# Scores computed a second time, transposed, with the row maxima contracted in, in place of transposed probabilities

## The reference

```
qkv = (h @ Wqkv.T).reshape(b, n, 3, H, HD)
q = _ln(qkv[:, :, 0].transpose(0, 2, 1, 3), qn_g, qn_b)
k = _ln(qkv[:, :, 1].transpose(0, 2, 1, 3), kn_g, kn_b)
v = qkv[:, :, 2].transpose(0, 2, 1, 3)
scores = jnp.einsum('bhnd,bhmd->bhnm', q, k) / jnp.sqrt(jnp.float32(HD))
attn = jax.nn.softmax(scores, axis=-1)
o = jnp.einsum('bhnm,bhmd->bhnd', attn, v)
x = x + o.transpose(0, 2, 1, 3).reshape(b, n, H * HD) @ Wout.T
```

## Time and profile before

| | |
|---|---|
| median of 3 runs | 466.15 us (465.32 to 466.54) |
| profiled execution | 464.51 us |
| its span, first to last instruction | 462.8 us |
| PE busy | 421.9 us, 91% |
| ACT, DVE, POOL busy | 311.0, 295.8, 154.8 us |
| mean granted TensorE clock | 0.978 of full |

### The profile page before, as it was taken

One profiled execution on the slowest core, in us unless ns is written; L12 is line 12 of the kernel. 1 busy time (PEld: TensorE's weight loads), 2 busy tenths in 40 slices (PEclk: granted clock), 3 DMA queues, 4 the chain that ended last, 5 costly groups with the idle time before them and its releaser, 6 DMA issues.

```text
span 462.8 us, 9105 instructions
## 1 busy us (share of the span) xinstructions
PE 421.9 (91%) x2990; PEld 366.4 (79%) x2990; DVE 295.8 (64%) x727; ACT 311.0 (67%) x697; POOL 154.8 (33%) x127
## 2 busy tenths in 40 slices
PE   1979878769999999999999999999999986889996
PEld 1567557658998998999999899999998875668794
DVE  2555545547776777677767767776776554886233
ACT  2345626566878887887788788778877766765531
POOL 6200313126553455355345535543553200100000
PEclk9999999889999999999999999999999999599999
DMA  7400000191000000000000000000000000000001
GB/s 212 131 1 1 2 0 1 32 339 39 1 4 0 1 1 0 0 0 0 0 0 0 0 0 0 0 0 0 0 0 2 1 0 2 0 1 1 1 1 45
DMA packets 7492, 9.49 MB, mean 21 GB/s; under 512 B 371, under 2 KB 4270, under 8 KB 7470
## 3 DMA queue, kind: packets, MB, share of 16 engines
q1 hardware_dynamic: 5646, 7.11, 5.1%
q10 hardware_dynamic: 1824, 2.10, 1.6%
HBM read 8.68 MB, written 0.52 MB: 20 GB/s over the span
## 4 chain that ended last, share of the span: by engine, by line
PE 71%; DVE 5%; issue 1%; ACT 1%; POOL 1%; DVEq 0%; ACTq 0%
PE pair L1349 24%; PE bank L1130 12%; PE pair L1315 8%; PE pair L1333 6%; PE pair L1334 6%; PE pair L1130 5%; PE pair L1539 1%; PE pair L1445 1%; PE pair L1484 1%; PE pair L1520 1%; PE bank L1484 1%; PE pair L1501 1%; PE pair L1528 1%; PE bank L1528 1%; PE bank L1520 1%
## 5 line engine op out<-in xcount | busy, mean ns | idle before, releaser
L1349 PE MATMUL pair<-v_s,probs_T 128*128 128x128 f32 x1024 | 135.5, 275 | 2.7 <-ACT probs_T L631 1.9
L936 DVE TENSOR_REDUCE negmax<-pair 128x1 f32<-128x512 f32 x128 | 88.1, 689 | 73.7 <-PE pair L1334 73.7
L1349 PEld LDWEIGHTS pair<-v_s,probs_T 128*128 128x128 f32 x1024 | 126.4, 192 | 6.5 <-issue 3.9
L631 ACT ACTIVATE probs_T<-bank 128x512 f32<-128x512 f32 x128 | 76.7, 599 | 45.7 <-PE bank L1130 45.7
L625 ACT ACTIVATE probs<-pair,negmax 128x512 f32<-128x512 f32 x128 | 88.3, 690 | 18.1 <-DVE negmax L936 18.1
L451 POOL TENSOR_TENSOR qk_rstd<-qk_ms,minus_half 128x8 f32<-128x8 f32 x32 | 54.6, 1706 | 134.0 <-DVE qk_ms L898 132.8
L1130 PE MATMUL bank<-ident,probs 128*128 128x128 f32 x512 | 77.4, 274 | 0.0
L1130 PEld LDWEIGHTS bank<-ident,probs 128*128 128x128 f32 x512 | 63.1, 141 | 12.9
L1333 PE MATMUL pair<-k_s,q_s 128*128 128x512 f32 x128 | 61.0, 477 | 3.3 <-ACT probs L625 3.3
L1334 PE MATMUL pair<-k_low,q_s 128*128 128x512 f32 x128 | 50.8, 397 | 0.0
L461 POOL TENSOR_TENSOR q_s<-kq,k_s 64x512 fp32r<-64x512 f32 x30 | 41.3, 1375 | 18.1 <-DVE k_s L913 13.3
(11 more groups left out here) (266 smaller groups left out, 644.0 us busy)
## 6 DMA issues: line engine op xcount, KB each, us to landing
fc_raw<-in_L_cond_fc2s_dram SPq DMA_DIRECT2D x1, 2048.0 KB, 14.6
x_in<-in_x_dram ACTq DMA_DIRECT2D x1, 512.0 KB, 3.8
w<-in_L_cond_mlp_w_dram SPq DMA_DIRECT2D x2, 256.0 KB, 3.6
wout<-in_L_cond_Wout_dram SPq DMA_DIRECT2D x1, 512.0 KB
b_all<-in_L_cond_b2s_dram SPq DMA_DIRECT2D x1, 512.0 KB, 10.3
out_dram<-final SPq DMA_DIRECT2D x2, 256.0 KB, 2.4
film<-in_L_cond_film_w_dram SPq DMA_DIRECT2D x2, 128.0 KB, 5.7
wq<-in_L_cond_q_w_dram SPq DMA_DIRECT2D x1, 64.0 KB, 7.7
```

What stands on the lines that cost most here:

```text
L631: act.activation(probs_T[:, c % 2, :, :].rearrange("p c n -> p (c n)"), bank[2 + c % 2][:, :], ACT.Copy).then_inc(probs_copied, 1)
L936: dve.tensor_reduce(negmax[:, s:s + 1], bank[s % 2][:, :], AX, ALU.max, negate=True)\
L1349: last = pe.matmul(bank[4][:, c * D:c * D + D], probs_T[:, c % 2, k, :], v_s[:, slot, k, :], start=(k == 0), stop=(k == NC - 1))
```

## The change

The probabilities are no longer transposed. A unit's scores are computed as before but with one matmul a chunk, q against k's high part alone (`scores`), only to get the row maxima; all four go to bank 0, one after the other, each behind the maximum of the one before. Then four small products (`shifts`: negmax spread over 128 columns as weights, against an identity) turn the four columns of negated maxima into one row of 512, and ACT copies that row into partition 64 of a new tile q_shift, whose first 64 partitions hold q's high part. `scores_T` computes the scores again with keys as rows, in two matmuls for each 128 keys: k_s as weights against q_s, and k_low, with a row of ones in partition 64, against q_shift, so that the maximum comes off in the sum. ACT takes the exponential from PSUM with no bias and no sum (`keys_exp`) and its output is what `mix` needs. v_s gets a column of ones, so that `mix` (129 columns now) also gives the sum.

So a unit runs over three: its maxima in time u, its transposed scores, exponentials and first three mixes in time u + 1, its fourth mix and output in time u + 2. `project(u + 4)` stands behind the fourth `scores` of unit u, then `shifts`, then the third mix of unit u - 1. On DVE `piece_norm(u + 3)` becomes the last step of a time, behind all four maxima and `k_high_beside` (which was called `piece_low`). ACT takes over from DVE the copy of q's high part, and has a second copy of it into q_shift and the copy of the row. Tiles for q and k hold three pairs of pieces instead of two; the loop is 12 units long and runs twice; the constant fills move on POOL behind the first layer's bias sum.

```diff
-                wait(act, probsT_done, g - 1)
-                act.activation(probs[:, c % 2, :], bank[c % 2][:, :], ACT.Exp, bias=negmax[:, c:c + 1],
-                               accum_out=row_sum[:, j % 2, c:c + 1]).then_inc(exp_done, 1)
+            def keys_exp(u, k):
+                wait(act, st_done, 4 * u + k + 1)
+                wait(act, pv_done, 4 * u + k - 1)
+                act.activation(probs_T[:, k % 2, :], bank[2 + k % 2][:, :], ACT.Exp).then_inc(exp_done, 1)
+            def copy_shift(u, r):
+                wait(act, shift_done, u + 1)
+                act.activation(q_shift[HD:HD + 1, r // 2 % PAIRS, r % 2, :], bank[1][HD:HD + 1, :], ACT.Copy)\
+                   .then_inc(shift_copied, 1)
...
+            def row_max(u, c):
+                wait(dve, s_done, 4 * u + c + 1)
+                if c == 0:
+                    wait(dve, shift_done, u)
+                dve.tensor_reduce(negmax[:, c:c + 1], bank[0][:, :], AX, ALU.max, negate=True).then_inc(max_done, 1)
...
+            def scores(u, r, c):
+                if c == 0:
+                    wait(pe, split_done, u + 2 - r % 2)
+                wait(pe, max_done, 4 * u + c)
+                pe.matmul(bank[0][:, :], q_s[:, pair_at, h, c * P:c * P + P], k_s[:, pair_at, h, :],
+                          start=True, stop=True).then_inc(s_done, 1)
+            def shifts(u, r):
+                wait(pe, max_done, 4 * u + 4)
+                for c in range(NC):
+                    last = pe.matmul(bank[1][:, c * P:c * P + P], negmax[:, c:c + 1].to_broadcast([P, P]),
+                                     ident_r[:, :], start=True, stop=True)
+                last.then_inc(shift_done, 1)
+            def scores_T(u, r, k):
+                wait(pe, exp_done, 4 * u + k - 1)
+                pe.matmul(bank[2 + k % 2][:, :], k_s[:, pair_at, h, at], q_s[:, pair_at, h, :], start=True, stop=False)
+                if k == 0:
+                    wait(pe, q_beside, u + 2 - r % 2)
+                    wait(pe, shift_copied, u + 1)
+                pe.matmul(bank[2 + k % 2][:, :], k_low[:, pair_at, h, at], q_shift[:, pair_at, h, :],
+                          start=False, stop=True).then_inc(st_done, 1)
```

More of the change, by code:

```diff
@@ L286, in piece_at, with turn_bank, pair_free, due @@
             half = p_in % 2 * (N // 2)
-            return t[lo:hi, p_in // 2 % 2, :, half:half + N // 2]
+            return t[lo:hi, p_in // 2 % PAIRS, :, half:half + N // 2]
         def kq_from(p):
[L291 to L312, removed]
+            return kq_second[:, :, :] if isinstance(p, int) and p == 1 else kq32[:, :, :]
+        def turn_bank(p):
+            return bank[3] if isinstance(p, int) and p < 2 else bank[1]
+        def pair_free(p, p_in):
+            return 4 * (p - 4) if p_in % 2 == 0 else 4 * (p - 5)
+        def due(u, lo, hi):
+            return not isinstance(u, int) or lo <= u <= hi
+        def every_time(eng, time):
+            for u in range(PER):
+                time(u, u, 0)
+            with eng.Fori(0, UNITS // RUN) as m:
+                for r in range(PER, PER + RUN):
+                    time(m * RUN + r, r, m * (RUN // PER) + r // PER)
+            for u in range(UNITS - PER, UNITS + 2):
+                time(u, u, u // PER)
         def attended(b):
-            return UNITS - (B - 1 - b) * PER // B
+            return 2 * (UNITS - (B - 1 - b) * PER // B)
         QK_BANKS, WOUT_BANKS, V_BANKS = 2 * KC // 4, KC // 4, H // 4
@@ L463, in piece_low, with time @@
                         .then_inc(lows_done, 1)
[L465 to L471, removed]
+            def time(u, r, i):
+                if due(u, 0, UNITS - 3):
+                    piece_low(u + 2, r + 2)
+                if due(u, 0, UNITS - 4):
+                    piece_scale(u + 3, u + 3)
             piece_scale(0, 0)
@@ L480, in _ @@
             piece_scale(2, 2)
[L481 to L484, removed]
+            every_time(pool, time)
             pool.wait_ge(tn_ss, TC)
@@ L657, in _ @@
             piece_affine(0)
[L658 removed]
+            q_high(0, 0)
             piece_affine(1)
@@ L993, in _ @@
             piece_norm(2, 2)
[L994 to L999 removed]
+            every_time(dve, time)
+            dve.wait_ge(o_normed, 2 * UNITS)
             for c in range(CANDS):
@@ new lines, in mix @@
+            def mix(u, r, k):
+                wait(pe, exp_done, 4 * u + k + 1)
+                if k == 0:
+                    wait(pe, v_placed, u + 2 - r % 2)
+                for c in range(NC):
+                    if k == 0 and c % 2 == 0:
+                        wait(pe, o_normed, 2 * u - 1 + c // 2)
+                    last = pe.matmul(pair4[:, c // 2, c % 2 * (D + 1):(c % 2 + 1) * (D + 1)],
+                                     probs_T[:, k % 2, c * P:c * P + P], v_s[:, r % (2 * PAIRS), k, :],
+                                     start=(k == 0 and c % 2 == 0), stop=(k == NC - 1 and c % 2 == 1),
+                                     skip_group_check=True)
+                last.then_inc(pv_done, 1)
```

314 lines of the change are left out of this document (147 added, 167 removed).

## The result

The changed kernel takes 591.35 us (median of 4 runs, 589.96 to 595.24) against 465.74 us before (4 runs, 464.93 to 466.54): a ratio of 1.2715, 95% interval 1.2669 to 1.2761. The forecast was 569 us with a range of 540 to 590. The side, the place of the loss and its mechanism held; the size fell short by 22 us, and the time lies just above the range.

A forecast was written before the change was run, and what follows sets the result against it. TensorE's own work bounded the kernel, 9.03 us a unit. Units of 11.64 us with opening and tail made the span 77.3 us longer, 543 us with the clock up; 26 us of clock falls made 569, range 540 to 590.

The forecast's parts named there:

- The side: Whole kernel: slower than before, given a chance of 0.97.
- the place of the loss: End of a unit: `project(u + 4)` was to wait most, 2.12 us, 2.22 with the restart.
- its mechanism: In the loop, TensorE waits for DVE's late norm and maxima, and its clock falls to 1.2 GHz behind pauses.
- TensorE's work: Per loop unit, TensorE's own work without waits falls by 0.36 us, to 8.67 from 9.03.
- The rival that this alone decides: Loop: the maximum's answer and the norm are both covered, 12 us less than before, 455 us; chance 0.02.
- The wait for the norm: End of a unit: 2.45 us from the fourth `scores` to `project`; TensorE waits 2.12, 2.22 with the restart.
- The wait for the maximum: Fourth `scores`, 1.17 us behind the third: waits 0.47 for its maximum in bank 0, 0.57 with the restart.
- The unit with the clock up: One loop unit without clock falls: 8.67 + 0.57 + 0.18 + 2.22 = 11.64 us, +2.63.
- The opening and the tail: Outside the loop: units 0 and 1 take 11.4 and 10.8 us, the last four 9.07 twice and 8.63 twice.
- The falls of the clock: Loop: TensorE's clock falls in 15 of 26 units, 1.7 us each, adding 26 us.
- The rival of nearly every unit: Loop: the clock falls in nearly every unit, 581 to 590 us; chance 0.13.
- What was late next: Behind the named waits: ACT's row copy, a unit's output and POOL's subtractions and power stay hidden, at no cost.

The follow-up runs named there:

- experiment 6: Changed kernel with the same work in another order on TensorE, DVE, ACT and POOL, no instruction added or taken away: 454.40 us.
- experiment 7: The reordered changed kernel (454.40 us) with its 24 loop units written out straight instead of a loop of 12 turning once: 450.76 us.
- Experiments 1: Changed kernel with `piece_norm(u + 3)` put back between DVE's third and fourth maximum: 506.88 us.
- 5: Kernel before with only `piece_norm` in the loop moved behind the fourth maximum and the copy: 556.23 us.
- experiment 2: Changed kernel with useless transposes of the identity ahead of `project`, in four groups, two or one: 552.80, 551.16 and 568.37 us.
- experiment 4: Changed kernel with scores for the maxima in two banks by turns: 560.74 us; with six useless transposes added too, 579.15 and 589.42 us in two executions.

## Why the prediction was right, and where it was not

**TensorE's work: right.** 8.67 a unit, 8.62 measured where nothing waits (6). The rival that this alone decides, 455 us, was refused because DVE's rows spoke against it; with the order changed so that they no longer do, 454 is measured. That the two agree to 1 us is in part luck, since the 454 contains the turn of the loop; without it the kernel takes 451 (7).

**The wait for the norm: right.** 2.45 from the fourth `scores` to `project` by rows of before; 2.45 and 2.57 in the two ends of the unit shown. Experiments 1 and 5 show that the norm's place is the cause: putting it back takes 84 us away, moving it in the kernel before adds 91.

**The wait for the maximum: right.** From the third to the fourth `scores` 1.26 instead of 1.17. Two banks make a unit 0.59 shorter; the prediction had 0.57. The Trainium skill (Perfetto Trace Analysis, Optimizing Tensor Performance, Matmuls) says to go round several banks; the runs agree, and by more than the sum had it: 31 us instead of 16, of which about 13 are falls of the clock that came less often.

**The unit with the clock up: 0.25 short.** 11.87, and 11.99 in every fourth unit, a mean of 11.89 (2), instead of 11.64. The fourth `scores` is 0.09 later, `project` 0.12 in every fourth unit, the four matmuls of `scores_T` ahead of the second `scores` take 0.08 more, and from there to the end of the first mix 0.14 more; `shifts` gives 0.05 back, and the other mixes a little. Times 26, that is 6.5 us. The kernel with its waits and no falls takes 552 us (2), where the prediction had 543: 6.5 of the 9 us are this term, and 1.9 the turn of the longer loop (13.8 instead of 11.9), which the sum did not have.

**The opening and the tail: right.** The third mix of unit 1's time was reckoned to end at 117.7; it does at 119.2 and 117.6 in the two kernels of experiment 2 without falls. The opening's 11.4 and 10.8 had no rows, so that is partly luck. The last units, from `shifts` to `shifts`, take 9.14 and 8.70 us; 9.07 and 8.63 were reckoned.

**The falls of the clock: the step that failed.** The price of one was about right, 1.58 us (2) against 1.7. Their number was not: "Not every pause need do so, so I take 15 of the 26 units", which was a middle between none and all, with no row for it. It is 24 of 26. The clock costs 591 - 552 = 39 us in place of 26, and these 13 with the 9 above are the 22 us missed. The rival of nearly every unit (581 to 590, 13 in 100) had the right count, and missed by the 9 us of the other term. The Trainium skill (TensorE: Matmul & The Clock Gate, A second HAM failure mode: psum-queue depth-cycling) describes a clock that goes down and up with short pauses between groups of matmuls; the trace agrees, at a rhythm of one fall in nearly each unit.

The prediction set the new pauses beside one that left the clock up and one that brought a fall. Such a pair says little, as the opening of the two kernels shows. Before, the clock stayed up behind a pause of 1.46 us that ended at 64.5, and fell behind that of 2.28 that ended at 86.5. In the changed kernel it fell at the first place, where the pause is again 1.46, and stayed up behind the second, where it is 2.20. Windows (us, PE busy, clock), one of before and two of the changed kernel:

```profile
65.00:66.00 1.00, 1.00 (x3) 1.00 0.00 0
```

```profile
65.00:66.00 1.00, 1.00 (x2) 0.50 0.00 0
87.00:88.00 1.00, 0.94 (x9) 1.00 0.00 0
```

The length of a pause alone does not decide whether the clock falls.

**What was late next: nothing.** The row that ACT copies, the output and POOL's power nowhere hold TensorE up in the changed kernel's loop beyond the named waits, but for 0.8 us behind the output at the loop's turn. The stall at the turn was missing from the sum; with falls in the units around it, it adds about 1 us (14.46 against 13.45), and 1.9 without.

## What to carry to other kernels

When work is moved between engines, follow the last step of each engine's round to who waits for it: a step that costs 0.7 us of an engine with half its time free cost 84 to 91 us by standing last. Price a pause of TensorE twice, by its length and by what its clock does behind it, and test the second by filling the pause with work that does nothing. How often the clock falls cannot be read from one pause that brought a fall and one that did not. A change that saves work but loses time may only stand in the wrong order: here the same instructions in another order take 454 us instead of 591.

## What the runs showed of the hardware that was not expected

Filling a pause with useless transposes made the kernel 39 us faster, where the prediction gave the clock 26. Pauses of TensorE of 1.1 us in each unit left its clock up in 26 units of 26; of 1.5 us, in 17; of 2.0 us, in 2 to 10, depending on the kernel, and what decides between these is not settled. Of one program the number differs between executions (579.15 and 589.42 us, experiment 4).

A loop of 12 units that turned once cost 0.7 to 4.4 us at the turn; in experiments 1 and 6 part of that is a fall of the clock. In experiment 6 engines stood up to 3.3 us without a releaser, while the DMA queues moved 8 GB/s. The packets of that stretch are on a queue that the page lists under instruction. The loop of 4 units of the kernel before turned five times with units of 9.01 to 9.02 us throughout, and from 165 to 349 us, in which these turns lie, its DMA queues moved nothing. With the code written out straight the stall was gone and nothing took its place (experiment 7). That instructions are loaded again at the turn fits all of this; no run shows it by itself.
